# One kernel, one convolution stage: weights loaded first, folding moved back, eight small casts, row statistics interleaved

## The chip, the core and the metric

One Trainium2 chip, one of its cores. The metric is the device time of one execution in microseconds (us). The engines are TensorE (PE: matmuls, and PEld: its weight loads), VectorE (DVE), ScalarE (ACT), GpSimd (POOL) and SyncE (SP), which here only issues DMAs. Engines run on their own and meet at semaphores.

## What is computed

An audio tower layer on x of 32 x 375 x 256: a strided convolution with a layer norm, then attention with a folded key/value projection, then a mixture of 16 experts beside a shared expert. The change is in the first part and in the preparation of weights for the others:

```python
xb = x.reshape(B, L // 2, 2, D)              # B 32, L padded to 376, D 256
h = einsum('btki,oik->bto', xb, conv_w) + conv_b + xb.mean(axis=2)
h = (h - mean) * rsqrt(var + 1e-5) * ln_gamma + ln_beta
h = h + attention(layernorm(h))              # k and v from ((W_k + W_v) @ W_down_kv) @ W_up_{k,v}
h = h + experts(layernorm(h)) + shared_expert(layernorm(h))
```

## The kernel before

Everything that matters to numbers is multiplied as a split of fp32 into two fp16 numbers: a high part (a copy scaled by 64 for weights) and a low part (the difference). A product takes three matmuls: high by high, low by high, high by low. ScalarE makes the high parts, GpSimd the low parts of the inputs, VectorE the low parts of the weights.

The convolution stage works on 32 batches of 188 rows, each in two tiles of 94 rows. Two batches, so four tiles, are a group g; there are 16 groups. Each tile has one of the eight PSUM banks, so even groups (par 0) use banks 0 to 3 and odd ones banks 4 to 7.

For each tile TensorE runs 13 matmuls (L1397, L1403): one for the bias row, twelve for four chunks of the contraction in three products. It waits for the low part of the batch (`xl_ready`) and until VectorE has read the bank two groups before (`gam_done`).

For each group the engines do, in the order of their programs:

- VectorE (`of_conv`, `of_normal`): four `bn_stats` of the PSUM tiles (L991), four `bn_aggr` (L985), then `stats_ready`; four scalar_tensor_tensor that subtract the mean and multiply by gamma (L999); a reciprocal (L1003). Then for the group two before, once GpSimd has added beta: four `bn_stats` of the normalized rows (L1010), four `bn_aggr`, and a copy of the result into `MV` (L1015). Groups 14 and 15 are done behind the loop.
- ScalarE (`conv_group`): the square root (L767), the high parts of two batches that are four ahead (`high_input`, L745), then, when the reciprocal is there, four scalings by it (L774).
- GpSimd: the low parts of the same two batches (`low_input`, L585), then the addition of beta into `H` (`add_beta`, L580).
- SyncE: the load of a batch into one of four input buffers, as soon as the low part of the batch before it there is made (L438).

Before the first group, SyncE issues constants, five weights of the folding, conv_w, bias, gamma and beta, four input batches, and the other weights, in that order. VectorE adds W_k and W_v, TensorE folds in two steps (L1378, L1383) through ScalarE, and only behind both does the first convolution tile start. VectorE adds half the identity to conv_w (L969), which gives the mean of the two rows.

The weights of the later stages are cast in two pieces. Behind its scalings in group 0 ScalarE makes the high part of 2048 columns, in group 1 that of 3104; VectorE makes the low parts behind its reciprocal of the same group (`low_weights`, L972). SyncE waits for both (`lo_done`) and issues, between the loads of inputs, blanks and tables that later stages need: they lie over the place of the uncast weights.

Of the kernel before, what the change touches and what calls it, by code (L numbers as in the profile page):

```python
# [49 lines left out]
HOT = FIRST + ROUNDS + 8  # L50
QE = 4
# [24 lines left out]
W_ALL = W_SD + 4 * D  # L76

# [28 lines left out]
def build(nc, x_t, conv_w, conv_b, gamma, beta, wq, wk_t, wv_t, wo, w_down, w_up_k, w_up_v, gate, s_g, s_u, s_d,  # L106
# [7 lines left out]
    with ctx:  # L114
# [130 lines left out]

        const_in, weights_in, fold_in, conv_w_in, bias_in = (sem(n) for n in ("const_in", "weights_in", "fold_in", "conv_w_in", "bias_in"))
# [61 lines left out]
        def conv_groups(eng, body):  # L308

            body(0, 0, 0)  # L310
            body(1, 1, 1)
            with eng.Fori(1, B // 4 - 1) as i:
                body(2 * i, 0, 2)
                body(2 * i + 1, 1, 2)
            body(B // 2 - 2, 0, 3)
            body(B // 2 - 1, 1, 3)
# [102 lines left out]
        def _(sp):  # L419
            sp.dma_start(C[:, :], const).then_inc(const_in, 16)  # L420
# [4 lines left out]
            sp.dma_start(WS[:, W_CONV:W_Q].rearrange("p (c n) -> p c n", c=4), conv_w.rearrange("(c p) n -> p c n", p=128)).then_inc(conv_w_in, 16)  # L425
            for dst, src in ((BIAS, conv_b), (GAM, gamma), (BET, beta)):
                sp.dma_start(dst, src.rearrange("(a n) -> a n", a=1).broadcast_to((128, D))).then_inc(bias_in, 16)
            for j in range(RING):
                sp.dma_start(XS[j], x_t[j, :, :]).then_inc(x_in[j], 16)
# [12 lines left out]
            sp.wait_ge(lo_done, 4)  # L442
            sp.wait_ge(fold_copied, 2)
            sp.dma_start(SEL, select).then_inc(blanks_in, 16)
            for par in range(2):
                sp.dma_start(MT[par], blank[:, 0:S]).then_inc(blanks_in, 16)
            for i in range(4, B // RING):
# [124 lines left out]
        def _(pool):  # L572
# [14 lines left out]
            def conv_group(g, par, age):  # L587
                if age < 3:
# [154 lines left out]
        def _(act):  # L743
# [3 lines left out]
            act.wait_ge(m1_done, 1)  # L747
            copy(M1[0:DL, :], bank[0][0:DL, 0:256]).then_inc(m1_copied, 1)
            for i in range(2):
                act.wait_ge(fold_done, i + 1)  # L750
                copy(WS[:, W_K + 512 * i:W_K + 512 * (i + 1)], bank[2 + i][:, :]).then_inc(fold_copied, 1)
            act.wait_ge(half_added, 4)
            copy(WH[:, W_CONV:W_Q], WS[:, W_CONV:W_Q], WSCALE).then_inc(hi_done, 1)
            act.wait_ge(bias_in, 16 * 3)
            act.wait_ge(rows_set, 2)
            copy(BROW[0:1, :], BIAS[0:1, :], WSCALE)
            copy(BHI[32:33, :], BIAS[32:33, :], WSCALE).then_inc(hi_done, 1)
# [7 lines left out]
            def conv_group(g, par, age):  # L765
                act.wait_ge(stats_ready, g + 1)
                nc.scalar.activation(SDB[par][0:HT, :], MVB[par][0:HT, :, 1], ACT.Sqrt, bias=C[0:HT, C_EPS64:C_EPS64 + 1]).then_inc(sd_done, 1)  # L767
                if age < 3:
# [12 lines left out]
            for j in range(RING):  # L781
                high_input(j, j)
            act.wait_ge(fold_copied, 2)
# [175 lines left out]
        def _(dve):  # L959
# [3 lines left out]
            dve.wait_ge(fold_in, 16 * 5)  # L963
            nc.vector.tensor_tensor(WKT, WKT, WVT, ALU.add).then_inc(summed, 1)
            dve.wait_ge(conv_w_in, 16)
            dve.wait_ge(const_in, 16)
# [3 lines left out]
            def low_weights(c0, c1, count):  # L970
                dve.wait_ge(hi_done, count)
                nc.vector.scalar_tensor_tensor(WL[:, c0:c1], WS[:, c0:c1], WSCALE, WH[:, c0:c1], ALU.mult, ALU.subtract).then_inc(lo_done, 1)  # L972

            low_weights(W_CONV, W_Q, 1)
            dve.wait_ge(hi_done, 2)
            nc.vector.scalar_tensor_tensor(BROW[32:33, :], BIAS[32:33, :], WSCALE, BHI[32:33, :], ALU.mult, ALU.subtract).then_inc(lo_done, 1)

# [9 lines left out]
            def of_conv(g, par, age):  # L987
# [7 lines left out]
                if age >= 2:  # L995
                    dve.wait_ge(bet_done, g - 1)
# [8 lines left out]
            def of_normal(g):  # L1005
# [5 lines left out]
                aggregate(ln_chain, STATN, AGGR)  # L1011
                ln_chain.wait()
                keep = MV[0:HT, bass.ts(g, CG), :] if not isinstance(g, int) else MV[0:HT, CG * g:CG * g + CG, :]
                hold(dve)
                ln_chain.mark(nc.vector.tensor_copy(keep, AGGR[0:HT, :, :]))  # L1015

            def conv_group(g, par, age):
                of_conv(g, par, age)
                if age == 0:
                    low_weights(W_Q, W_GATE, 3)  # L1020
                if age == 1:
                    low_weights(W_GATE, W_ALL, 4)
                if age >= 2:
                    of_normal(g - 2)
# [3 lines left out]
            with dve.Fori(0, B // 4 - 1) as i:  # L1028
# [4 lines left out]
            conv_chain.leave(B // 4 - 1)  # L1033
            ln_chain.leave(B // 4 - 1)
            for g in (B // 2 - 2, B // 2 - 1):
                of_normal(g)
# [337 lines left out]
        def _(pe):  # L1374
            mm = nc.tensor.matmul
            pe.wait_ge(summed, 1)
            for c in range(2):
                last = mm(bank[0][0:DL, 0:256], WDN[:, c * DL:(c + 1) * DL], WKT[:, c * 256:(c + 1) * 256], start=c == 0, stop=c == 1)  # L1378
            last.then_inc(m1_done, 1)
            pe.wait_ge(m1_copied, 1)  # L1380
            for i, w_ in enumerate((WUK, WUV)):
                for c in range(2):
                    last = mm(bank[2 + i][:, c * 256:(c + 1) * 256], M1[0:DL, c * 128:(c + 1) * 128], w_[0:DL, :], start=True, stop=True)  # L1383
                last.then_inc(fold_done, 1)

            pe.wait_ge(fold_copied, 2)
            pe.wait_ge(lo_done, 2)
            with pe.Fori(0, B // 4) as i:
                for par in range(2):
                    for j in range(2):  # L1390
                        pe.wait_ge(xl_ready, 4 * i + 2 * par + j + 1)
                        xh, xl = XH[2 * par + j], XL[2 * par + j]
                        for qt in range(2):
                            t = 2 * j + qt
                            pe.wait_ge(gam_done, 2 * CG * i + CG * par + t + 1)
                            to = bank[CG * par + t][0:HT, 0:D]
                            mm(to, ONE16, BROW, start=True, stop=False)  # L1397
                            n = 0
                            for c in range(4):
                                w = slice(W_CONV + c * D, W_CONV + (c + 1) * D)  # L1400
                                x = slice(c * S + qt * HT, c * S + (qt + 1) * HT)
                                for a, w_ in split3(xh[:, x], xl[:, x], WH[:, w], WL[:, w]):
                                    last = mm(to, a, w_, start=False, stop=n == 11)  # L1403
                                    n += 1
                            last.then_inc(conv_done, 1)
# [381 lines left out]
```

## Time and profile before

| | |
|---|---|
| time, median of 3 runs | 1866.77 us (1864.56 to 1869.98) |
| span of the profiled execution, first to last instruction | 1863.2 us |
| TensorE busy, of the span | 1690.4 us (91%) |
| VectorE, GpSimd, ScalarE busy | 1227.8, 949.9, 903.4 us |
| convolution stage, its last VectorE copy ends | 148.96 us |
| mean granted TensorE clock | 0.961 |

The profiled execution's own time is given only as its span; the three runs were timed without the profiler. An instruction row of a timeline gives the start in us from the span's start, the duration in us, engine, line, operation, what it writes and reads with partitions x elements, how many were merged (xN), and in brackets how long the engine was idle before and what ended that.

### The profile page before, as it was taken

The page shows a single profiled execution, that of the slowest core. Times are in us where ns is not written, and L with a number is a line of the kernel's source. Part 1 is how long each engine was busy: PE and PEld are TensorE (multiplying, and loading weights), DVE is VectorE, ACT ScalarE, POOL GpSimd, SP SyncE. Part 2 cuts the span into 40 slices and gives each one's busy share as a digit, 9 for nine tenths or more (in the row PEclk, how much of TensorE's full clock was granted, in tenths as well). Part 3 has the DMA queues.
Part 4 walks back from the last instruction along what each step waited for, and adds up shares of the span by engine and source line. Part 5 has one row for each costly group of instructions (what it writes and reads, how often), then busy time and mean ns, then how long its engine had stood idle before and what let it go on. Part 6 is the DMA issues. An engine that isn't in the chain of part 4 may idle for free.

```text
span 1863.2 us, 46732 instructions
## 1 busy us (share of the span) xinstructions
PE 1690.4 (91%) x15566; PEld 1233.5 (66%) x15566; DVE 1227.8 (66%) x3755; ACT 903.4 (48%) x1965; POOL 949.9 (51%) x945
## 2 busy tenths in 40 slices
PE   6874899999999998579999679999999999999997
PEld 5873566666666665357777557777777777777775
DVE  3883778888888888475778665555555555555551
ACT  4442556666666665344234454444444444444442
POOL 3771244444444443372224244666666666666675
PEclk9995999999999999889999779999999999999999
DMA  5532555555655565242110152333333333343422
GB/s 183 171 106 46 110 121 118 133 124 131 126 135 121 133 134 123 59 128 48 34 32 28 42 182 84 100 103 102 99 93 93 99 97 100 102 102 99 101 34 28
DMA packets 220233, 186.52 MB, mean 100 GB/s; under 512 B 165624, under 2 KB 200952, under 8 KB 214008
## 3 DMA queue, kind: packets, MB, share of 16 engines
q1 hardware_dynamic: 193272, 141.11, 28.7%
q0 software_dynamic: 26880, 44.36, 11.6%
q8 instruction: 48, 0.79, 0.2%
q14 instruction: 33, 0.27, 0.1%
HBM read 134.49 MB, written 50.44 MB: 99 GB/s over the span
## 4 chain that ended last, share of the span: by engine, by line
PE 66%; DVE 9%; issue 8%; POOL 5%; SPq 4%; DMA 4%; ACT 1%; DVEq 0%; POOLq 0%; ACTq 0%
PE psum L1698 26%; PE psum L1715 14%; PE psum L1563 6%; PE psum L1583 4%; SPq L466 3%; DVE arena L1101 3%; DVE psum L1109 2%; PE psum L1519 2%; PE psum L1462 2%; PE psum L1416 2%; PE psum L1484 2%; DMA arena<-inverse_sums 2%; PE psum L1430 2%; POOL hidden L580 2%; POOL arena L585 1%
## 5 line engine op out<-in xcount | busy, mean ns | idle before, releaser
L644 POOL TENSOR_TENSOR arena<-arena 128x376 f16<-128x376 f32 x320 | 316.8, 992 | 352.9 <-ACT arena L745 351.4
L1698 PE MATMUL psum<-arena,hidden 128*128 128x376 f16 x3072 | 493.8, 323 | 0.9 <-DVE arena L1337 0.9
L1698 PEld LDWEIGHTS psum<-arena,hidden 128*128 128x128 f16 x3072 | 301.2, 98 | 189.4 <-issue 2.3
L745 ACT ACTIVATE arena<-arena 128x376 f16<-128x376 f32 (+5 forms) x610 | 287.2, 474 | 55.7 <-DVE arena L1273 45.7
L1101 DVE CUSTOM_DVE_ANT_0 arena<-psum,constants 128x188 f32<-128x188 f32 x768 | 227.8, 345 | 107.8 <-PE psum L1416 106.5
L941 ACT ACTIVATE arena<-psum 128x376 f32<-128x376 f32 x256 | 123.9, 484 | 342.7 <-PE psum L1698 342.7
L745 ACT ACTIVATE arena<-psum 128x188 f32<-128x188 f32 (+7 forms) x457 | 168.5, 399 | 237.1 <-PE psum L1678 58.0
L1347 DVE SCALAR_TENSOR_TENSOR arena<-psum,arena 128x376 f32<-128x376 f32 x256 | 140.7, 550 | 185.4 <-ACT arena L941 184.0
L1715 PE MATMUL psum<-hidden,arena 128*128 128x256 f16 (+1 forms) x2304 | 256.6, 273 | 0.0
L1715 PEld LDWEIGHTS psum<-hidden,arena 128*128 128x128 f16 (+1 forms) x2304 | 229.9, 103 | 21.7
L1329 DVE SCALAR_TENSOR_TENSOR hidden<-arena,hidden 128x512 f16<-128x512 f32 x192 | 210.1, 1098 | 8.8 <-ACT hidden L745 8.8
L794 ACT ACTIVATE arena<-psum 128x564 f32<-128x564 f32 x256 | 164.1, 641 | 102.9 <-PE psum L1430 101.4
L602 POOL TENSOR_TENSOR arena<-arena 128x376 f16<-128x376 f32 x128 | 115.5, 902 | 170.7 <-ACT arena L745 164.9
L1109 DVE TENSOR_TENSOR psum<-psum,constants 128x564 f32<-128x564 f32 x256 | 191.1, 747 | 7.4 <-PE psum L1441 7.3
L690 POOL DMA_INDIRECT out<-hidden,arena x96 | 149.8, 1561 | 45.2 <-DVE hidden L1357 23.1
L1357 DVE TENSOR_SCALAR hidden<-psum,arena 128x256 f32<-128x256 f32 x96 | 46.3, 482 | 164.8 <-PE psum L1715 164.5
L1563 PE MATMUL psum<-arena,weights_hi 128*128 128x376 f16 x512 | 136.9, 328 | 1.2 <-DVE arena L1140 1.2
L1430 PE MATMUL psum<-arena 128*128 128x188 f16 x768 | 106.1, 247 | 26.6 <-DVE psum L1109 20.6
L1462 PE MATMUL psum<-arena 128*32 128x188 f32 (+1 forms) x2048 | 125.2, 332 | 4.6 <-ACT arena L794 0.8
L1416 PE MATMUL psum<-arena 96*128 96x188 f16 x768 | 108.3, 251 | 23.3 <-DVE arena L1101 14.3
L681 POOL DMA_INDIRECT arena<-token_table,arena x96 | 110.5, 1151 | 26.8 <-POOL arena L674 11.9
L745 ACT ACTIVATE hidden<-arena 128x512 f16<-128x512 f32 x192 | 118.3, 620 | 5.9 <-DMA arena<-e_g 3.6
(156 smaller groups left out, 2651.4 us busy)
## 6 DMA issues: line engine op xcount, KB each, us to landing
arena<-q_halves SPq DMA_DIRECT2D x384, 47.0 KB, 2.5
arena<-k_halves SPq DMA_DIRECT2D x384, 47.0 KB, 2.3
arena<-e_g SPq DMA_DIRECT2D x16, 1024.0 KB
arena<-e_u SPq DMA_DIRECT2D x16, 1024.0 KB, 5.1
arena<-e_d SPq DMA_DIRECT2D x16, 1024.0 KB
arena<-x_t SPq DMA_DIRECT2D x32, 376.0 KB, 3.5
weighed<-arena POOLq DMA_DIRECT2D x32, 376.0 KB, 4.0
q_halves<-arena SPq DMA_DIRECT2D x32, 188.0 KB, 3.3
```

The costliest lines, as they stand in the source:

```text
L644: nc.gpsimd.tensor_tensor(dst, f, hi, ALU.subtract).then_inc(ready, 1)
L690: nc.gpsimd.indirect_dma_start(out[:, :], bass.IndirectOffsetOnAxis(ap=IDXS[par][0:n, m:m + 1], axis=0), EO[par][0:n, m * D:(m + 1) * D], ...
L745: return nc.scalar.activation(dst, src, ACT.Copy, scale=scale)
L794: nc.scalar.activation(PT[i % RING], TB[i % 2], ACT.Exp).then_inc(exp_done, 1)
L1101: last = nc.vector.tensor_tensor_reduce(out=SC[t], in0=SB[t], in1=C[:, C_DECAY + t * S:C_DECAY + (t + 1) * S], scale=1.0, scalar=-3e38, op ...
L1109: nc.vector.tensor_tensor(TB[j % 2], TB[j % 2], C[:, C_DECAY:C_DECAY + 3 * S], ALU.mult).then_inc(multiplied, 1)
L1329: nc.vector.scalar_tensor_tensor(WEL[par][:, c], WST[:, c], WSCALE, WEH[par][:, c], ALU.mult, ALU.subtract).then_inc(wl_ready[i], 1)
L1416: last = mm(SB[t], QD[cpar][0:2 * KR, i * CW + t * 128:i * CW + (t + 1) * 128], KX[cpar][0:2 * KR, i * S:(i + 1) * S], start=True, stop=True)
L1462: last = mm(OB[32 * k:32 * k + 32, :], V[cpar][p0:p0 + rows, v:v + 32], PT[a % RING][p0:p0 + rows, t * S:(t + 1) * S], start=n == 0, stop= ...
L1563: last = mm(bank[2 * (m % 2) + i][:, 0:CHUNK], w_, a, start=n == 0, stop=n == 5)
L1698: last = mm(bank[2 * (s % 2) + i][:, 0:CHUNK], w_, a, start=n == 0, stop=n == 5)
L1715: last = mm(bank[down_bank[m]][0:rows, 0:D], a, w_, start=n == 0, stop=n == 23)
```

## The change

- SyncE issues only the identity columns of the constants first (new semaphore `ident_in`), then batch 0, conv_w, bias, gamma, beta, batches 1 to 3, the rest of the constants, the folding's weights, and the others. value_rows goes with the first blanks; the wait for the casts moves behind the loads of i == 5, ahead of the blanks for QD and KD.
- The folding goes behind the first group's matmuls, in banks 6 and 7, in three pieces between tiles of group 1. ScalarE keeps the results in group 0.
- The 5152 other columns are cast in `CASTS = 8` pieces of 644, one in each of the groups 2 to 9 (age 2).
- VectorE issues the `bn_stats` and `bn_aggr` of the normalized rows right behind those of the convolution, ahead of the gamma pass. The copy into `MV` becomes a maximum of AGGR with itself and stands between the gamma pass and the reciprocal.

```diff
 SyncE
-            sp.dma_start(C[:, :], const).then_inc(const_in, 16)
+            sp.dma_start(C[:, C_ID:C_ONES], const[:, C_ID:C_ONES]).then_inc(ident_in, 16)
+            sp.dma_start(XS[0], x_t[0, :, :]).then_inc(x_in[0], 16)
+            sp.dma_start(WS[:, W_CONV:W_Q].rearrange("p (c n) -> p c n", c=4), conv_w.rearrange("(c p) n -> p c n", p=128)).then_inc(conv_w_in, 16)
...
             for i in range(4, B // RING):
                 load_x(i)
-                for par in range(2):
-                    v = (*QD, *KD, *V)[2 * (i - 4) + par] if i < 7 else None
-                    if v is not None:
-                        sp.dma_start(v, value_rows if i == 6 else blank).then_inc(blanks_in, 16)
+                if i == 5:
+                    sp.wait_ge(lo_done, 2 + CASTS)
+                if i in (5, 6):
+                    for v in (QD, KD)[i - 5]:
+                        sp.dma_start(v, blank).then_inc(blanks_in, 16)
 ScalarE, conv_group
+                if age == 0:
+                    keep_fold(0)
                 act.wait_ge(inv_ready, g + 1)
                 for t in range(CG):
                     v = LN[par][0:HT, t * D:(t + 1) * D]
                     nc.scalar.activation(v, v, ACT.Copy, scale=RSB[par][0:HT, t:t + 1]).then_inc(scale_done, 1)
-                if age == 0:
-                    act.wait_ge(weights_in, 16 * 6)
-                    copy(WH[:, W_Q:W_GATE], WS[:, W_Q:W_GATE], WSCALE).then_inc(hi_done, 1)
-                if age == 1:
-                    copy(WH[:, W_GATE:], WS[:, W_GATE:], WSCALE).then_inc(hi_done, 1)
+                if age == 0:
+                    keep_fold(1)
+                if age == 1:
+                    act.wait_ge(weights_in, 16 * 6)
+                    act.wait_ge(fold_copied, 2)
+                if age == 2:
+                    copy(WH[:, cast_columns(g)], WS[:, cast_columns(g)], WSCALE).then_inc(hi_done, 1)
 VectorE
+            def normal_stats(g):
+
+                dve.wait_ge(bet_done, g + 1)
+                hold(dve)
+                for t in range(CG):
+                    ln_chain.mark(nc.vector.bn_stats(STATN[t][0:HT, :], H[0:HT, CG * g + t, :]))
+
+            def keep_normal(g):
+
+                keep = MV[0:HT, bass.ts(g, CG), :] if not isinstance(g, int) else MV[0:HT, CG * g:CG * g + CG, :]
+                ln_chain.wait()
+                hold(dve)
+                ln_chain.mark(nc.vector.tensor_tensor(keep, AGGR[0:HT, :, :], AGGR[0:HT, :, :], ALU.max))
+
+            def conv_group(g, par, age):
                 for t in range(CG):
                     dve.wait_ge(conv_done, CG * g + t + 1)
                     hold(dve)
                     conv_chain.mark(nc.vector.bn_stats(STAT[t][0:HT, :], bank[CG * par + t][0:HT, 0:D]))
+                if age >= 2:
+                    normal_stats(g - 2)
                 aggregate(conv_chain, STAT, MVB[par])
+                if age >= 2:
+                    aggregate(ln_chain, STATN, AGGR)
                 conv_chain.wait()
                 dve.sem_inc(stats_ready, 1)
...
                                                    GAM[0:HT, :], ALU.subtract, ALU.mult).then_inc(gam_done, 1)
+                if age >= 2:
+                    keep_normal(g - 2)
                 dve.wait_ge(sd_done, g + 1)
                 hold(dve)
                 nc.vector.reciprocal(RSB[par][0:HT, :], SDB[par][0:HT, :]).then_inc(inv_ready, 1)
...
+                if age == 2:
+                    low_weights(cast_columns(g), g + 1)
 TensorE
+            pe.wait_ge(lo_done, 2)
+            for t in range(CG):
+                conv_tile(0, 0, t)
+            fold_first()
+            for t in range(CG):
+                if t >= 2:
+                    pe.wait_ge(fold_copied, t - 1)
+                conv_tile(0, 1, t)
+                if t < 2:
+                    fold_second(t)
+            with pe.Fori(1, B // 4) as i:
                 for par in range(2):
+                    for t in range(CG):
+                        conv_tile(i, par, t)
```

## Rows read from the trace of the kernel before

**Rows 1.** Timeline of VectorE at the stage's end (columns as above).
```profile
134.46 2.12 DVE L1015 COPY mean_var<-arena 94x8 f32 x1 [0.24 <-DVE arena L985]
...
138.05 0.38 DVE L985 BATCH_NORM_AGGREGATE arena<-arena 94x2 f32<-94x6 f32 x4
...
148.79 0.17 DVE L1015 COPY mean_var<-arena 94x8 f32<-94x8 f32 x1
```

**Rows 2.** Timeline of GpSimd in a steady group.
```profile
95.90 2.34 POOL L580 TENSOR_TENSOR hidden<-arena 94x1024 f32 x1
99.06 3.18 POOL L585 TENSOR_TENSOR arena<-arena 128x752 f16<-128x752 f32 x2 [0.82 <-ACT arena L745]
```

**Rows 3.** Timeline of VectorE in the same group.
```profile
95.93 1.42 DVE L991 BATCH_NORM_STATS2 arena<-psum 94x6 f32<-94x256 f32 x4
...
98.13 1.66 DVE L999 SCALAR_TENSOR_TENSOR arena<-psum,arena 94x256 f32<-94x256 f32 x4 [0.26 <-DVE arena L985]
...
99.79 1.37 DVE L1010 BATCH_NORM_STATS2 arena<-hidden 94x6 f32 x4
...
101.93 0.34 DVE L1015 COPY mean_var<-arena 94x8 f32 x1 [0.24 <-DVE arena L985]
```

**Rows 4.** Timeline of GpSimd at the stage's end.
```profile
134.22 2.34 POOL L580 TENSOR_TENSOR hidden<-arena 94x1024 f32<-94x1024 f32 x1 [3.82 <-ACT arena L774]
```

**Rows 5.** Chain that ended last, one tile of group 15 (start, us, what).
```profile
126.95 1.32 PE psum L1403 x12
```

**Rows 6.** Timeline of VectorE: aggregates of groups 0 to 2 and the weight casts.
```profile
28.55 0.38 DVE L985 BATCH_NORM_AGGREGATE arena<-arena 94x2 f32<-94x6 f32 x4
...
35.52 3.57 DVE L972 SCALAR_TENSOR_TENSOR weights_lo<-arena,weights_hi 128x2048 f16<-128x2048 f32 x1 [4.55 <-ACT weights_hi L745]
...
40.58 0.38 DVE L985 BATCH_NORM_AGGREGATE arena<-arena 94x2 f32<-94x6 f32 x4
...
47.38 3.50 DVE L972 SCALAR_TENSOR_TENSOR weights_lo<-arena,weights_hi 128x3104 f16<-128x3104 f32 x1 [4.45 <-ACT weights_hi L745]
...
52.36 0.38 DVE L985 BATCH_NORM_AGGREGATE arena<-arena 94x2 f32<-94x6 f32 x4
```

**Rows 7.** Timeline of GpSimd beside those casts.
```profile
34.59 2.35 POOL L580 TENSOR_TENSOR hidden<-arena 94x1024 f32<-94x1024 f32 x1
...
45.28 2.36 POOL L580 TENSOR_TENSOR hidden<-arena 94x1024 f32<-94x1024 f32 x1
```

**Rows 8.** Timeline of all engines, from the start to the first convolution matmul.
```profile
3.95 0.58 SPq L425 DMA_DIRECT2D arena<-conv_w  x1
...
7.83 1.97 PE L1378 MATMUL psum<-arena 128*64 128x256 f32 x4 [7.83 <-DVE arena L964]
...
8.77 0.90 DVE L969 SCALAR_TENSOR_TENSOR arena<-constants,arena 128x128 f32<-128x128 f32 x4 [0.99 <-DMA arena<-conv_w]
...
10.27 3.77 PE L1383 MATMUL psum<-arena 64*128 64x256 f32 x8 [0.47 <-ACT arena L745]
...
15.65 1.23 DVE L972 SCALAR_TENSOR_TENSOR weights_lo<-arena,weights_hi 128x1024 f16<-128x1024 f32 x1 [5.99 <-ACT weights_hi L745]
...
19.02 0.44 PE L1397 MATMUL psum<-arena 128*94 128x256 f16 x1 [4.98 <-POOL arena L585]
```

**Rows 9.** Timeline of ScalarE: high parts of weights.
```profile
14.57 1.05 ACT L745 ACTIVATE weights_hi<-arena 128x1024 f16<-128x1024 f32 x1
...
33.59 1.90 ACT L745 ACTIVATE weights_hi<-arena 128x2048 f16<-128x2048 f32 x1
```

**Rows 10.** Timeline of ScalarE in the steady group of rows 2 and 3.
```profile
97.97 0.30 ACT L767 ACTIVATE arena<-arena,constants 94x4 f32<-94x4 f32 x1 [2.58 <-DVEq L994]
98.17 1.53 ACT L745 ACTIVATE arena<-arena 128x752 f16<-128x752 f32 x2
99.90 1.70 ACT L774 ACTIVATE arena<-arena 94x256 f32<-94x256 f32 x4 [0.20 <-DVE arena L1003]
```

**Rows 11.** DMA issues of the first 150 us (KB each, median us to landing).
```profile
arena<-blank SPq DMA_DIRECT2D x4, 768.0 KB, 5.8
```

More of the change, by code:

```diff
@@ L50 @@
 HOT = FIRST + ROUNDS + 8
+CASTS = 8
 QE = 4
@@ L76 @@
 W_ALL = W_SD + 4 * D
+CAST = (W_ALL - W_Q) // CASTS
+assert CAST * CASTS == W_ALL - W_Q
 class Chain:
@@ L243, in meet @@
             eng.wait_ge(engines_met, met[id(eng)])
+        ident_in = sem("ident_in")
         const_in, weights_in, fold_in, conv_w_in, bias_in = (sem(n) for n in ("const_in", "weights_in", "fold_in", "conv_w_in", "bias_in"))
@@ L311, in conv_groups, with cast_columns @@
             body(1, 1, 1)
-            with eng.Fori(1, B // 4 - 1) as i:
+            with eng.Fori(1, 1 + CASTS // 2) as i:
                 body(2 * i, 0, 2)
                 body(2 * i + 1, 1, 2)
-            body(B // 2 - 2, 0, 3)
-            body(B // 2 - 1, 1, 3)
+            with eng.Fori(1 + CASTS // 2, B // 4 - 1) as i:
+                body(2 * i, 0, 3)
+                body(2 * i + 1, 1, 3)
+            body(B // 2 - 2, 0, 4)
+            body(B // 2 - 1, 1, 4)
+        def cast_columns(g):
+            return bass.ds(W_Q + CAST * (g - 2), CAST)
         def hsplit(ap):
@@ L419, in _ @@
         def _(sp):
-            sp.dma_start(C[:, :], const).then_inc(const_in, 16)
+            sp.dma_start(C[:, C_ID:C_ONES], const[:, C_ID:C_ONES]).then_inc(ident_in, 16)
+            sp.dma_start(XS[0], x_t[0, :, :]).then_inc(x_in[0], 16)
+            sp.dma_start(WS[:, W_CONV:W_Q].rearrange("p (c n) -> p c n", c=4), conv_w.rearrange("(c p) n -> p c n", p=128)).then_inc(conv_w_in, 16)
+            for dst, src in ((BIAS, conv_b), (GAM, gamma), (BET, beta)):
+                sp.dma_start(dst, src.rearrange("(a n) -> a n", a=1).broadcast_to((128, D))).then_inc(bias_in, 16)
+            for j in range(1, RING):
+                sp.dma_start(XS[j], x_t[j, :, :]).then_inc(x_in[j], 16)
+            sp.dma_start(C[:, C_ONES:C_ALL], const[:, C_ONES:C_ALL]).then_inc(const_in, 16)
             for dst, src in ((WKT, wk_t), (WVT, wv_t), (WDN, w_down)):
@@ L424, in _ @@
             sp.dma_start(WUV[0:DL, :], w_up_v).then_inc(fold_in, 16)
[L425 to L429, printed above, removed]
             for o, src, c in ((W_Q, wq, 2), (W_O, wo, 2)):
@@ L441, in _ @@
                 load_x(i)
-            sp.wait_ge(lo_done, 4)
             sp.wait_ge(fold_copied, 2)
@@ L587, in conv_group @@
             def conv_group(g, par, age):
-                if age < 3:
+                if age < 4:
                     for j in range(2):
@@ L745, in copy, with keep_fold @@
                 return nc.scalar.activation(dst, src, ACT.Copy, scale=scale)
-            act.wait_ge(m1_done, 1)
-            copy(M1[0:DL, :], bank[0][0:DL, 0:256]).then_inc(m1_copied, 1)
-            for i in range(2):
+            def keep_fold(i):
                 act.wait_ge(fold_done, i + 1)
[L751 to L757, printed above, removed]
+                copy(WS[:, W_K + 512 * i:W_K + 512 * (i + 1)], bank[6 + i][:, :]).then_inc(fold_copied, 1)
             def high_input(b, j):
@@ L775, in conv_group @@
                 if age == 0:
+                    keep_fold(1)
+                if age == 1:
                     act.wait_ge(weights_in, 16 * 6)
-                    copy(WH[:, W_Q:W_GATE], WS[:, W_Q:W_GATE], WSCALE).then_inc(hi_done, 1)
-                if age == 1:
-                    copy(WH[:, W_GATE:], WS[:, W_GATE:], WSCALE).then_inc(hi_done, 1)
-            for j in range(RING):
+                    act.wait_ge(fold_copied, 2)
+                if age == 2:
+                    copy(WH[:, cast_columns(g)], WS[:, cast_columns(g)], WSCALE).then_inc(hi_done, 1)
+            high_input(0, 0)
+            act.wait_ge(half_added, 4)
+            copy(WH[:, W_CONV:W_Q], WS[:, W_CONV:W_Q], WSCALE).then_inc(hi_done, 1)
+            act.wait_ge(bias_in, 16 * 3)
+            act.wait_ge(rows_set, 2)
+            copy(BROW[0:1, :], BIAS[0:1, :], WSCALE)
+            copy(BHI[32:33, :], BIAS[32:33, :], WSCALE).then_inc(hi_done, 1)
+            for j in range(1, RING):
                 high_input(j, j)
-            act.wait_ge(fold_copied, 2)
+            act.wait_ge(m1_done, 1)
+            copy(M1[0:DL, :], bank[7][0:DL, 0:256]).then_inc(m1_copied, 1)
             conv_groups(act, conv_group)
@@ L961, in _ @@
                 dve.sem_inc(s_, v_)
-            dve.wait_ge(fold_in, 16 * 5)
-            nc.vector.tensor_tensor(WKT, WKT, WVT, ALU.add).then_inc(summed, 1)
             dve.wait_ge(conv_w_in, 16)
-            dve.wait_ge(const_in, 16)
+            dve.wait_ge(ident_in, 16)
             for c in range(4):
@@ L1003, in of_conv @@
                 nc.vector.reciprocal(RSB[par][0:HT, :], SDB[par][0:HT, :]).then_inc(inv_ready, 1)
-            def of_normal(g):
-                dve.wait_ge(bet_done, g + 1)
-                hold(dve)
-                for t in range(CG):
-                    ln_chain.mark(nc.vector.bn_stats(STATN[t][0:HT, :], H[0:HT, CG * g + t, :]))
[L1011 to L1018, printed above, removed]
-                if age == 0:
[L1020 to L1024, printed above, removed]
+                if age == 2:
+                    low_weights(cast_columns(g), g + 1)
             conv_group(0, 0, 0)
             conv_group(1, 1, 1)
-            with dve.Fori(0, B // 4 - 1) as i:
+            with dve.Fori(0, CASTS // 2) as i:
                 conv_chain.enter(i, 4 * CG)
@@ L1032, in _ @@
                 conv_group(2 * i + 3, 1, 2)
-            conv_chain.leave(B // 4 - 1)
-            ln_chain.leave(B // 4 - 1)
-            for g in (B // 2 - 2, B // 2 - 1):
-                of_normal(g)
+            conv_chain.leave(CASTS // 2)
+            ln_chain.leave(CASTS // 2)
+            with dve.Fori(0, B // 4 - 2 - CASTS // 2) as i:
+                conv_chain.enter(i, 4 * CG)
+                ln_chain.enter(i, 4 * CG + 2)
+                conv_group(2 * i + 2 + CASTS, 0, 3)
+                conv_group(2 * i + 3 + CASTS, 1, 3)
+            conv_chain.leave(B // 4 - 2 - CASTS // 2)
+            ln_chain.leave(B // 4 - 2 - CASTS // 2)
+            for g in (B // 2 - 2, B // 2 - 1):
+                conv_group(g, g % 2, 4)
+            for g in (B // 2 - 2, B // 2 - 1):
+                normal_stats(g)
+                aggregate(ln_chain, STATN, AGGR)
+                keep_normal(g)
             ln_chain.wait()
@@ L1375, in _ @@
             mm = nc.tensor.matmul
[L1376 to L1381, printed above, removed]
-                for c in range(2):
-                    last = mm(bank[2 + i][:, c * 256:(c + 1) * 256], M1[0:DL, c * 128:(c + 1) * 128], w_[0:DL, :], start=True, stop=True)
-                last.then_inc(fold_done, 1)
@@ L1386, in _, with fold_first @@
-            pe.wait_ge(fold_copied, 2)
-            pe.wait_ge(lo_done, 2)
-            with pe.Fori(0, B // 4) as i:
-                for par in range(2):
[L1390 to L1405, printed above, removed]
+            def fold_first():
+                pe.wait_ge(summed, 1)
+                for c in range(2):
+                    last = mm(bank[7][0:DL, 0:256], WDN[:, c * DL:(c + 1) * DL], WKT[:, c * 256:(c + 1) * 256], start=c == 0, stop=c == 1)
+                last.then_inc(m1_done, 1)
@@ new lines, in fold_second, with conv_tile @@
+            def fold_second(i):
+                pe.wait_ge(m1_copied, 1)
+                for c in range(2):
+                    last = mm(bank[6 + i][:, c * 256:(c + 1) * 256], M1[0:DL, c * 128:(c + 1) * 128], (WUK, WUV)[i][0:DL, :], start=True, stop=True)
+                last.then_inc(fold_done, 1)
+            def conv_tile(i, par, t):
+                j, qt = divmod(t, 2)
+                if qt == 0:
+                    pe.wait_ge(xl_ready, 4 * i + 2 * par + j + 1)
+                xh, xl = XH[2 * par + j], XL[2 * par + j]
+                pe.wait_ge(gam_done, 2 * CG * i + CG * par + t + 1)
+                to = bank[CG * par + t][0:HT, 0:D]
+                mm(to, ONE16, BROW, start=True, stop=False)
+                n = 0
+                for c in range(4):
+                    w = slice(W_CONV + c * D, W_CONV + (c + 1) * D)
+                    x = slice(c * S + qt * HT, c * S + (qt + 1) * HT)
+                    for a, w_ in split3(xh[:, x], xl[:, x], WH[:, w], WL[:, w]):
+                        last = mm(to, a, w_, start=False, stop=n == 11)
+                        n += 1
+                last.then_inc(conv_done, 1)
```

15 lines of the change are left out of this document (8 added, 7 removed).

## The prediction

> **What bounds the kernel now.** The change touches only the convolution stage, which ends at 148.96 us of the 1863.2 us span (the last copy of [rows 1]); what follows stays as it is, so the sum is made over these 149 us. I read three things: the stage's start, the two groups with a large weight cast, and a steady group, each as an engine's timeline.
>
> A steady group takes 6.3 us here: GpSimd adds beta from 95.90 and has the next group's low inputs done, and is free for the next addition, at 99.06 + 3.18 = 102.24 [rows 2]. In [rows 3] VectorE is nearly always at work: statistics of the convolution, gamma pass, statistics of the normalized rows. The last row shows what closes the cycle: a copy of 94x8 values takes 0.34 us and ends at 102.27, just when those low inputs have ended [rows 2]. In [rows 1] the same copy takes 2.12 us and ends at 136.58; GpSimd's operation of [rows 4] ends at 136.56. It waits for GpSimd to be done. TensorE is nearly as full: a tile is 1.32 us of twelve matmuls and 0.11 of the bias one, so 5.7 us a group [rows 5].
>
> The same hold is seen on the weight casts [rows 6, 7]. The 2048-column low part starts at 35.52 and ends at 39.09; GpSimd's addition ends at 36.94, and 2.15 us remain, 1.05 ns a column. The 3104-column one ends at 50.88, 3.24 us after GpSimd's 47.64, again 1.04 ns. With GpSimd idle, 1024 columns took 1.23 us [rows 8]. So a VectorE operation with two inputs in SBUF stands still while GpSimd's runs. Before it VectorE had waited 4.55 and 4.45 us for ScalarE: ScalarE casts only after scaling its four tiles. From aggregate to aggregate these groups took 12.03 and 11.78 us (28.93, 40.96, 52.74, [rows 6]).
>
> I write M(g) for the end of the convolution's aggregates in group g. Before: M(0) = 28.93, M(2) = 52.74, M(15) = 138.43, stage end 10.53 later.
>
> **Start: earlier weights.** conv_w was issued at 3.95, and its first use was at 8.77 [rows 8], 4.8 us later. Now it is third in SyncE's queue, issued near 1.8; between 4.0 and 4.8 us to landing I take 4.3: 6.1. Then as before: identity added 0.90, high part 1.05 [rows 9], low part 1.23 [rows 8], about 0.4 for the bias row and 0.2 of hand-overs: TensorE starts at 9.9 instead of 19.02. Cold start and first group took 28.93 - 19.02 = 9.9, so M(0) = 19.8.
>
> **Folding moved.** It comes behind the first group. Its twelve fp32 matmuls took 1.97 + 3.77 us at the 1.2 GHz level [rows 8]; now TensorE is at its 2.4 GHz level and I take half, 2.9. Group 1 then ends on TensorE at 18.7 + 2.9 + 5.7 = 27.3, and its aggregates 1.1 later. ScalarE, which first keeps M1 and then both folds between its own steps, is ready for the last tile at about the same time. I take M(1) = 28.6. Group 2 adds 5.7 of TensorE, the last statistic and 1.37 of row statistics, and the aggregates: M(2) = 35.8. Bounds 33 to 39. So at M(2) the new kernel is 16.9 us ahead: 9.1 from the start, the rest because groups 0 and 1 no longer cast.
>
> **The eight small casts.** Groups 2 to 9 each cast 644 columns. Their order is that of before: in one group ScalarE scales four tiles, casts, and only then VectorE forms the low part; the next group's statistics are queued behind it on VectorE, and TensorE's banks and ScalarE's square root behind those. Step by step from M:
> - gamma pass to 1.6 (1.66 with its overlap, no pause before it now) [rows 3];
> - ScalarE: square root at -0.1, high inputs to 1.6, which lets GpSimd's two low inputs run from 1.0 to 2.6 and on to 4.2, as [rows 2, 10] lie now;
> - the operation that replaces the copy, a maximum of two SBUF inputs, arrives at 1.65. Held by the first low input it ends at 2.7. Bounds: 0.1 unheld, and both low inputs, 2.6. I take 1.0, since the copy, too, got in between two GpSimd operations that stood back to back. Unheld, beta would start at 4.2, when the low inputs end, instead of 4.7 as below: 0.5 less in eight groups and 0.6 in the four late ones, 6 in all, 1881;
> - reciprocal 2.8, ScalarE's scaling to 4.6 (1.70, [rows 10]), cast 0.73 (1.05 - 380 x 0.83 ns, the slope of [rows 9]) to 5.3;
> - GpSimd adds beta from 4.7 to 7.0 (2.35, [rows 2]). The cast's low part arrives at 5.3, is held to 7.0, and takes 0.67 more: 7.7. Unheld it would end at 6.15;
> - convolution statistics, row statistics, two sets of aggregates: 1.35 + 1.37 + 0.75, now without pauses: M(g+1) = M(g) + 11.2.
>
> That is the pattern of the two old casts (12.03 and 11.78), now eight times, and the narrow width saves little since the order and the hold cost most. M(10) = 35.8 + 8 x 11.2 = 125.4. TensorE idles half of each such group. If it falls to 1.2 GHz for a whole group, that is twice 5.7 = 11.4 us, and it runs a group ahead: hidden, except in the rival below.
>
> **Groups from 10 on.** SyncE now waits for the eighth cast before it issues two 768 KB blanks and, behind them, the inputs of group 10. The cast ends at M(9) + 7.7, 3.5 us before M(10). A blank lands in 5.8 us [rows 11], and the input follows: ScalarE gets it some 3.3 us late. GpSimd, TensorE and VectorE follow, and TensorE restarts after a pause. Over two groups I take 17.2 instead of 12.6 us, 4.6 lost (bounds 0 and 8). Groups 12 and 13: the hold remains, pauses go: 2.8 + 1.35 + 1.37 + 0.75 = 6.3 each. Group 14 loads no input, so the maximum goes unheld: 5.4. M(15) = 125.4 + 17.2 + 12.6 + 5.4 = 160.6.
>
> **Tail.** Both last row statistics still wait for GpSimd's beta, and one maximum is held by it: 8.4 instead of 10.5 us ([rows 1]: 138.43 to 148.96). Stage end 169.0.
>
> **Sum.** Three pieces: -16.9 us at M(2); from M(2) to M(15) 160.6 - 35.8 = 124.8 against 138.43 - 52.74 = 85.7, so +39.1; tail -2.1. Together +20.1 us, and the stage ends at 169.0. The span becomes 1883; the median of the runs shown lies 3.6 us above the profiled span, so 1866.8 + 20 = 1887 us.
>
> **Rivals.**
> - *Held nowhere, and the blanks hidden (faster).* If two-input operations run beside GpSimd, the maximum costs 0.1, and a cast group is 1.85 + 1.7 + 0.73 + 0.85 + 3.5 = 8.6. Eight of them give back 20.8 us, the late groups 2.4: 1864, or 1859 if the blanks hide as well. The place is the cast groups; below 8.7 us each the change breaks even, below 8.0 it is measurably faster. Against it: both ends in [rows 6] fit GpSimd's end within 0.02 us.
> - *Starved.* If the maximum waits for both low inputs, 1.6 us more in twelve groups: +19, 1906 us. For it: GpSimd's two stand back to back. Against: the copy got in.
> - *Blanks hidden, holds as forecast.* 4.6 less: 1882.
> - *TensorE slow.* It falls to 1.2 GHz between cast groups and then sets the end of some: 3 to 6 us more, 1890 to 1893.
> - That the change moves nothing would need the cast groups to come at 8.7 us, 2.1 over the mean of before (85.7 / 13 = 6.6); the fixed order alone (scaling, cast, low part) puts VectorE 3.3 us behind its reciprocal.
>
> **How the numbers follow.** Forecast 0.60; held nowhere 0.11 (0.04 faster, 0.07 within the bound); starved 0.09; blanks hidden 0.12; TensorE slow 0.08. About 0.3% (5.6 us) is what a measurement here can tell from no change. To allow for an unseen mistake in the cast groups I move 0.03 from slower to faster and 0.01 to same. Range 1872 to 1899: the forecast with the start's bounds of 3, half a microsecond on each cast group and the blanks' bounds, the hidden blanks and the slow TensorE, 0.60 + 0.12 + 0.08 = 0.8 in all; left out are the held-nowhere case below and the starved one above.
>
> **What would show it.** TensorE's first convolution matmul near 10 us; low parts of 644 columns that last about 2.4 us and end 0.67 after GpSimd's addition; aggregates 11 us apart in groups 2 to 9; maxima of about 1 us; after the eighth cast two blanks and a late input; the stage's end near 169. The prediction is wrong if the low parts last 0.8 us, if ScalarE's cast precedes its scaling, or if the cast groups come at 8 us.

## The result and the profile after

The changed kernel takes 1884.11 us (median of 4 runs, 1880.26 to 1888.71), the kernel before on the same chip 1866.93: ratio 1.0099, 95% interval 1.0082 to 1.0115. It is slower, as forecast: +20 us was forecast, the medians lie 17.2 us apart, and by the ratio it is 18.5. The profiled span is 1886.7 us. The stage ends at 168.49 us, forecast 169.0, before 148.96 [rows 1]; the 19.5 us between the two are, within some 2 us, the whole loss.

First VectorE's timeline in groups 2 and 3, which answers to [rows 6] (start, us, then as before; M(g) is, as in the prediction, the end of the convolution's aggregates in group g):

```profile
37.14 0.62 DVE L1005 BATCH_NORM_AGGREGATE arena<-arena 94x2 f32<-94x6 f32 x8
...
39.34 1.00 DVE L1019 TENSOR_TENSOR mean_var<-arena 94x8 f32 x1
...
43.09 2.30 DVE L988 SCALAR_TENSOR_TENSOR weights_lo<-arena,weights_hi  x1 [2.66 <-ACT weights_hi L759]
...
47.95 0.61 DVE L1005 BATCH_NORM_AGGREGATE arena<-arena 94x2 f32<-94x6 f32 x8
```

M(2) is 37.76, M(3) 48.56: 10.8 us. VectorE stands idle 2.66 us for ScalarE's cast, and the low part then lasts 2.30 us. The timelines of ScalarE and of GpSimd say why:

```profile
37.81 1.53 ACT L759 ACTIVATE arena<-arena 128x752 f16<-128x752 f32 x2
40.46 1.71 ACT L782 ACTIVATE arena<-arena 94x256 f32<-94x256 f32 x4 [1.11 <-DVE arena L1041]
42.07 0.73 ACT L759 ACTIVATE weights_hi<-arena  x1
```

```profile
38.71 3.18 POOL L599 TENSOR_TENSOR arena<-arena 128x752 f16<-128x752 f32 x2 [1.27 <-ACT arena L759]
42.35 2.35 POOL L594 TENSOR_TENSOR hidden<-arena 94x1024 f32 x1 [0.47 <-ACT arena L782]
```

ScalarE's cast waits behind its scalings. VectorE's low part then arrives at 43.09, inside GpSimd's addition; the addition ends at 44.70, and the low part 0.69 us later. The maximum starts 0.63 us into GpSimd's first low input and ends at 40.34, when that one is done. The eight groups 2 to 9 are alike. The list of waits from 40 to 120 us (waiting line, releaser: us in total, times, longest) has the wait for the cast, but not the hold, which is inside the low part's duration:

```profile
DVE weights_lo L988 <- ACT weights_hi L759: 21.1, 8, 2.7
```

TensorE works 62 of these 87 us, at a mean granted clock of 0.82, and runs ahead: VectorE is not once seen waiting for it between 40 and 120 us. The row gives the stretch, its length, then busy us and count of PE, PEld, DVE, ACT and POOL, the clock, the DMA share and GB/s:

```profile
37.80:124.40 86.60, 62.44 (x445) 59.44 (x444) 65.26 (x184) 32.45 (x65) 44.14 (x24) 0.82 0.27 83
```

Where the eighth cast ends (120.92), SyncE issues the blanks and, behind them, the inputs of group 10; ScalarE then gets the input late. TensorE stands idle for 6.75 us, and from 131 to 135 us its granted clock is 0.50, the 1.2 GHz level: the first two tiles behind the pause take 2.80 and 2.04 us, the next ones 1.42. VectorE waits for these tiles, so 2.0 us of the 17.4 from M(10) to M(12) are the lower clock's; this is read from the trace, no run isolates it. Two maxima show both ends of the hold: at 126.08 GpSimd is idle and the maximum takes 0.15 us, and in group 13 it takes 2.71 us. Timelines of SyncE, ScalarE, GpSimd and VectorE, one fence each:

```profile
120.95 0.80 SPq L466 DMA_DIRECT2D arena<-blank  x2
121.79 2.09 SPq L451 DMA_DIRECT2D arena<-x_t  x4
```

```profile
128.84 1.75 ACT L759 ACTIVATE arena<-arena 128x752 f16<-128x752 f32 x2 [4.18 <-DMA arena<-x_t]
```

```profile
148.78 3.19 POOL L599 TENSOR_TENSOR arena<-arena 128x752 f16<-128x752 f32 x2
```

```profile
126.08 0.15 DVE L1019 TENSOR_TENSOR mean_var<-arena 94x8 f32 x1
...
149.27 2.71 DVE L1019 TENSOR_TENSOR mean_var<-arena 94x8 f32 x1
...
168.33 0.16 DVE L1019 TENSOR_TENSOR mean_var<-arena 94x8 f32<-94x8 f32 x1
```

At the start, TensorE's first convolution matmul is at 11.18 us (19.02 before, [rows 8]). The four identity additions, which have two inputs in SBUF, now fall beside GpSimd's first low input, which was not so before. Timelines of VectorE and of GpSimd:

```profile
6.20 1.82 DVE L985 SCALAR_TENSOR_TENSOR arena<-constants,arena 128x128 f32<-128x128 f32 x4 [6.20 <-DMA arena<-conv_w]
```

```profile
5.66 1.60 POOL L599 TENSOR_TENSOR arena<-arena 128x752 f16<-128x752 f32 x1 [4.48 <-ACT arena L759]
```

Taken one by one, the first addition lasts 1.21 us, the other three 0.28 each. The low input ends at 7.26, and the additions 0.76 us behind it: they were held too. In the profiles of all eight experiments, which share this start, the distance is 0.75 or 0.76 us again, while the low input itself starts anywhere from 5.19 to 5.88.

### The profile page after: what moved, and what is told of

It is laid out like the page before. It is cut to its first block, busy times and chain, and to the rows that moved or that the text cites. A ratio compares the mean times of both kernels' runs of the same rounds, so it can differ in the third digit from the quotient of the medians.

```text
span 1886.7 us, 46738 instructions
## 1 busy us (share of the span) xinstructions
PE 1700.6 (90%) x15566; PEld 1241.9 (66%) x15566; DVE 1245.2 (66%) x3761; ACT 903.7 (48%) x1971; POOL 948.2 (50%) x945
## 4 chain that ended last, share of the span: by engine, by line
PE 70%; DVE 13%; issue 7%; DMA 3%; SPq 2%; ACT 2%; POOL 2%; DVEq 1%; POOLq 0%; ACTq 0%
PE psum L1744 26%; PE psum L1761 13%; PE psum L1609 6%; PE psum L1629 4%; DVE arena L1131 3%; DVE psum L1139 3%; PE psum L1508 3%; PE psum L1565 2%; PE psum L1434 2%; PE psum L1476 2%; PE psum L1462 2%; PE psum L1530 2%; PE psum L1487 2%; SPq L480 1%; PE psum L1724 1%
## 5 line engine op out<-in xcount | busy, mean ns | idle before, releaser
L759 ACT ACTIVATE arena<-arena 128x376 f16<-128x376 f32 (+4 forms) x610 | 287.8, 474 | 66.2 <-DVE arena L1303 46.5
L1761 PEld LDWEIGHTS psum<-hidden,arena 128*128 128x128 f16 (+1 forms) x2304 | 230.0, 103 | 21.6
L1139 DVE TENSOR_TENSOR psum<-psum,constants 128x564 f32<-128x564 f32 x256 | 191.1, 746 | 10.8 <-PE psum L1487 10.6
```

The source lines that it names most:

```text
L759: return nc.scalar.activation(dst, src, ACT.Copy, scale=scale)
L1139: nc.vector.tensor_tensor(TB[j % 2], TB[j % 2], C[:, C_DECAY:C_DECAY + 3 * S], ALU.mult).then_inc(multiplied, 1)
L1761: last = mm(bank[down_bank[m]][0:rows, 0:D], a, w_, start=n == 0, stop=n == 23)
```

## The experiments

Ratios are to the kernel before on the same chip; two chips were used, and their medians for the kernel before differ by 3.4 us (1864.84 for the first four experiments, 1868.26 for the other four), so times are compared here through the ratios. For each run the stage's end is given too (148.96 before, 168.49 changed).

**The casts undone.** Behind ScalarE's scalings, and the like on VectorE; SyncE's wait ahead of the blanks becomes one for 4, so the blanks no longer come late either:

```diff
                 if age == 0:
                     keep_fold(1)
-                if age == 1:
                     act.wait_ge(weights_in, 16 * 6)
                     act.wait_ge(fold_copied, 2)
-                if age == 2:
-                    copy(WH[:, cast_columns(g)], WS[:, cast_columns(g)], WSCALE).then_inc(hi_done, 1)
+                    copy(WH[:, W_Q:W_GATE], WS[:, W_Q:W_GATE], WSCALE).then_inc(hi_done, 1)
+                if age == 1:
+                    copy(WH[:, W_GATE:], WS[:, W_GATE:], WSCALE).then_inc(hi_done, 1)
```

> The eight small casts are undone: the other weights are cast in two pieces, 2048 columns in group 0 and 3104 in group 1, as in the kernel before; start, folding, row statistics and maximum stay as changed. Theory (each cast puts its group some 4.4 us behind, by the order scaling, cast, low part and by GpSimd's hold): groups 0 and 1 get longer, M(2) near 47 instead of 37.8, but groups 2 to 9 come at about 6.3 us instead of 10.8; stage end 136 to 140 instead of 168.5, time 1852 to 1856, faster than both. Rival (the loss sits in the interleaved statistics and the maximum, not in the casts): the groups stay near 10 us and the time stays over 1875.

Measured: 1864.35 us, 0.9999 (0.9988 to 1.0010), stage end 147.60. The loss of the changed kernel is gone, so it sat in the eight casts and what hangs on them; but the forecast gain did not come. M(2) is 47.38 as expected, and then most groups take 7.5 us, not 6.3 (M(14) is 134.34, so 7.25 in the mean of twelve). VectorE's timeline of groups 3 and 4, and GpSimd's, show it:

```profile
52.57 0.62 DVE L1005 BATCH_NORM_AGGREGATE arena<-arena 94x2 f32<-94x6 f32 x8
...
54.76 2.70 DVE L1019 TENSOR_TENSOR mean_var<-arena 94x8 f32 x1
...
60.21 0.62 DVE L1005 BATCH_NORM_AGGREGATE arena<-arena 94x2 f32<-94x6 f32 x8
```

```profile
51.96 2.35 POOL L594 TENSOR_TENSOR hidden<-arena 94x1024 f32 x1 [0.47 <-ACT arena L782]
54.27 3.17 POOL L599 TENSOR_TENSOR arena<-arena 128x752 f16<-128x752 f32 x2
```

The maximum ends at 57.46, GpSimd's second low input at 57.44: the maximum was held by both, as in my rival "starved". Ten of the twelve maxima in the loops lasted 2.29 to 2.72 us.

**The cast ahead of the scalings.**

```diff
+                if age == 2:
+                    copy(WH[:, cast_columns(g)], WS[:, cast_columns(g)], WSCALE).then_inc(hi_done, 1)
                 act.wait_ge(inv_ready, g + 1)
                 for t in range(CG):
...
-                if age == 2:
-                    copy(WH[:, cast_columns(g)], WS[:, cast_columns(g)], WSCALE).then_inc(hi_done, 1)
```

> One line moved: ScalarE casts its 644 columns behind the two high inputs and ahead of the four scalings, where it idles 1.1 us for the reciprocal. Theory (fixed order costs most): VectorE's low part no longer waits for ScalarE, arrives 2.9 us behind M and is held only by GpSimd's second low input to 4.25, ends at 4.9 instead of 7.6: groups of 8.1 instead of 10.8 us, -21.6 us, 1862. Rival (the hold alone costs it): the low part would still end behind GpSimd's addition of beta, no gain beyond 2 us.

Measured: 1851.66 us, 0.9931 (0.9913 to 0.9948), stage end 135.69. It gains 33 us at the stage's end, more than the 21.6 expected. VectorE's timeline, then GpSimd's:

```profile
37.44 0.62 DVE L1005 BATCH_NORM_AGGREGATE arena<-arena 94x2 f32<-94x6 f32 x8
...
39.64 1.00 DVE L1019 TENSOR_TENSOR mean_var<-arena 94x8 f32 x1
40.65 0.79 DVE L988 SCALAR_TENSOR_TENSOR weights_lo<-arena,weights_hi  x1
...
44.01 0.62 DVE L1005 BATCH_NORM_AGGREGATE arena<-arena 94x2 f32<-94x6 f32 x8
```

```profile
39.01 3.90 POOL L599 TENSOR_TENSOR arena<-arena 128x752 f16<-128x752 f32 x2 [1.28 <-ACT arena L759]
```

The group takes 6.57 us. I had the low part held by the second low input; instead it runs in 0.79 us right behind the maximum and the reciprocal, and the second low input waits for it: GpSimd's two last 3.90 us instead of 3.18. The edit takes away both the wait for the cast and the hold by beta; the next experiment takes away the hold alone. The order is right as a cause; who holds whom I had wrong.

**Beta behind the low part.**

```diff
                 if age < 4:
                     for j in range(2):
                         low_input(2 * g + RING + j, 2 * par + j)
+                if age == 2:
+                    pool.wait_ge(lo_done, g + 1)
                 add_beta(g, par)
```

> In groups 2 to 9 GpSimd waits for VectorE's low part of the weights before it adds beta; nothing else. Theory (a two-input operation of VectorE stands still beside GpSimd): the low part takes 0.85 us instead of 2.31, groups of 9.3 instead of 10.8, -12 us, 1872. Rival (2.3 us is what such a strided operation of 644 columns costs by itself): it stays at 2.3 us, beta comes later, and the time is the same or up to 5 us longer.

Measured: 1871.04 us, 1.0028 (1.0015 to 1.0041), stage end 156.78. As the theory had it: the low part takes 0.83 us beside an idle GpSimd, and M to M is 9.3 us.

```profile
43.02 0.83 DVE L990 SCALAR_TENSOR_TENSOR weights_lo<-arena,weights_hi  x1 [2.66 <-ACT weights_hi L761]
...
46.40 0.62 DVE L1007 BATCH_NORM_AGGREGATE arena<-arena 94x2 f32<-94x6 f32 x8
```

So the hold is 1.5 us a group, some 12 us in all, and the wait for the cast, 2.66 us, is still there. The two together, 4.2 us, are what moving the cast took off a group (10.8 to 6.57).

**One input instead of two.**

```diff
-                ln_chain.mark(nc.vector.tensor_tensor(keep, AGGR[0:HT, :, :], AGGR[0:HT, :, :], ALU.max))
+                ln_chain.mark(nc.vector.tensor_reduce(keep, AGGR[0:HT, :, :].unsqueeze(3), AX.X, ALU.max))
```

> The maximum of AGGR with itself becomes a tensor_reduce over an axis of length one: same result, one input. Theory (two inputs make it wait for GpSimd): 0.1 to 0.2 us instead of 1.0 (2.7 once); in the cast groups beta then starts when the low inputs end, 0.45 earlier, 3.6 us in all; some 2 to 3 us more in groups 12 and 13; 1878. Rival (eight values in a register-addressed tile cost 1 us whatever the form): no change.

Measured: 1877.86 us, 1.0072 (1.0049 to 1.0094), stage end 163.92, 4.6 less than changed. The operation takes 0.15 us in the same place, and the low part, now 2.68 us, waits for the same addition of beta, which starts a little earlier:

```profile
39.23 0.15 DVE L1019 TENSOR_REDUCE mean_var<-arena 94x8 f32 x1
...
42.11 2.68 DVE L988 SCALAR_TENSOR_TENSOR weights_lo<-arena,weights_hi  x1 [2.65 <-ACT weights_hi L759]
```

Groups 12 and 13 now take 5.7 us each. So the eight values wait as a tensor_tensor of two inputs and not as a tensor_reduce of one. One input alone is not the rule: the copy of the kernel before has one input too, and was held for 2.12 us [rows 1, 4].

**The blanks spread.** Each blank is issued once the pieces of weights under it are cast:

```diff
-                if i == 5:
-                    sp.wait_ge(lo_done, 2 + CASTS)
-                if i in (5, 6):
-                    for v in (QD, KD)[i - 5]:
+                if i >= 5:
+                    for v, pieces in (((QD[0], 1), (QD[1], 4)), ((KD[0], 6),), ((KD[1], 8),))[i - 5]:
+                        sp.wait_ge(lo_done, 2 + pieces)
                         sp.dma_start(v, blank).then_inc(blanks_in, 16)
```

> The changed kernel, but the four blanks for QD and KD no longer stand together behind the wait for the eighth cast: each is issued behind the loads of inputs once the pieces that lie under it are cast (1 and 4 pieces at i == 5, 6 at i == 6, 8 at i == 7). Theory (the blanks hold back the inputs of group 10 and TensorE pauses): from M(10) to M(12) some 12 to 13 us instead of 17.4; 4 to 5 us less, 1879 to 1880. Rival (that time is something else, such as the new loop that starts there): no change.

Measured: 1883.52 us, 1.0081 (1.0061 to 1.0100), stage end 164.14. By times alone it can't be told from the changed kernel (the intervals overlap). By the profiles M(10) to M(12) takes 13.5 us (123.93 to 137.40) instead of 17.4 (124.38 to 141.75), and ScalarE no longer waits there. One maximum in these two groups is held for 2.70 us, which takes back part of the gain. The 4 us are shown in the trace only.

**Start and folding alone.** Two casts, row statistics apart and the copy, as in the kernel before, in the new start. Of the edit, the part on the statistics:

```diff
-                if age >= 2:
-                    normal_stats(g - 2)
                 aggregate(conv_chain, STAT, MVB[par])
-                if age >= 2:
-                    aggregate(ln_chain, STATN, AGGR)
...
+                if age >= 2:
+                    of_normal(g - 2)
```

> The kernel before with only the new start, the folding behind the first group and its tables' DMAs: casts in two pieces, row statistics apart and the copy, all as before. Theory: TensorE starts near 11 us instead of 19, M(2) near 47.5 instead of 52.7, and steady groups of 6.46 us as before: 1860 to 1862, 5 us faster than before. If the interleaved statistics with a maximum held 2.7 us every other group are a loss, it is 2 to 4 us faster than e1_two_casts (1864). Rival (the interleaving helps by its fewer pauses): slower than e1_two_casts.

Measured: 1859.55 us, 0.9948 (0.9928 to 0.9968), stage end 141.55. M(2) is 45.38 instead of 52.74, and that 7.4 us is kept to the stage's end. The gain by time, 9 us, is more than the 5 expected; M(2) had come 2 us earlier than expected. Against the two-cast version above the stage ends 6 us earlier: interleaved statistics with a held maximum are a loss.

**The three mended together.** Cast ahead of the scalings, tensor_reduce, blanks spread; of the three diffs above, the lines that carry them:

```diff
+                if age == 2:
+                    copy(WH[:, cast_columns(g)], WS[:, cast_columns(g)], WSCALE).then_inc(hi_done, 1)
                 act.wait_ge(inv_ready, g + 1)
...
+                ln_chain.mark(nc.vector.tensor_reduce(keep, AGGR[0:HT, :, :].unsqueeze(3), AX.X, ALU.max))
...
+                    for v, pieces in (((QD[0], 1), (QD[1], 4)), ((KD[0], 6),), ((KD[1], 8),))[i - 5]:
```

> The changed kernel with three edits: cast ahead of the scalings, tensor_reduce instead of the maximum, blanks spread. Theory, added up from the parts: e2_cast_before_scaling at 1851.7; cast groups 6.3 instead of 6.57 us, -2; blanks -6; groups 12 and 13 at TensorE's 5.7, -2: 1842, 22 us faster than before. Rival (the gains overlap, since TensorE's 5.7 us is the floor): 1846.

Measured: 1844.68 us (1837.66 to 1846.98), 0.9860 (0.9833 to 0.9887), stage end 126.08. It beats both kernels. Its median lies between the theory's 1842 and the rival's 1846, but these were reckoned from times on the other chip. Against the kernel before on its own chip it is 23.6 us faster by the medians; the theory had 22, the rival some 19, which is a ratio of 0.990 and just outside the interval. So the theory is favoured, by a narrow margin. VectorE's timeline:

```profile
36.76 0.62 DVE L1004 BATCH_NORM_AGGREGATE arena<-arena 94x2 f32<-94x6 f32 x8
...
38.95 0.15 DVE L1018 TENSOR_REDUCE mean_var<-arena 94x8 f32 x1
...
39.89 0.83 DVE L987 SCALAR_TENSOR_TENSOR weights_lo<-arena,weights_hi  x1 [0.70 <-ACT weights_hi L758]
...
43.27 0.62 DVE L1004 BATCH_NORM_AGGREGATE arena<-arena 94x2 f32<-94x6 f32 x8
...
125.92 0.16 DVE L1018 TENSOR_REDUCE mean_var<-arena 94x8 f32<-94x8 f32 x1
```

Cast groups come at 6.5 us, not 6.3: the low part now waits 0.7 us for the cast.

**Two casts and one input.** The two-cast version, and

```diff
-                ln_chain.mark(nc.vector.tensor_tensor(keep, AGGR[0:HT, :, :], AGGR[0:HT, :, :], ALU.max))
+                ln_chain.mark(nc.vector.tensor_reduce(keep, AGGR[0:HT, :, :].unsqueeze(3), AX.X, ALU.max))
```

> e1_two_casts with the tensor_reduce instead of the maximum. Theory (e1 lost its gain to the maximum, held for 1.0 to 2.7 us in twelve groups; unheld, VectorE needs some 5.3 us a group and TensorE's 5.7 sets the pace): groups 2 to 13 of 5.7 instead of 7.25 us, -18 us, 1846. Rival (the groups of e1 are slow for another cause, such as the order of statistics and gamma pass): no change beyond 3 us.

Measured: 1847.52 us, 0.9889 (0.9871 to 0.9907), stage end 130.79. Most groups come at 5.68 us, TensorE's pace (VectorE's timeline):

```profile
59.42 0.62 DVE L1005 BATCH_NORM_AGGREGATE arena<-arena 94x2 f32<-94x6 f32 x8
...
65.10 0.62 DVE L1005 BATCH_NORM_AGGREGATE arena<-arena 94x2 f32<-94x6 f32 x8
```

VectorE now waits for TensorE's last tile, ten times up to 0.6 us between 60 and 120 us. The maximum alone was worth 16.8 us of stage there (147.60 to 130.79), where groups are tight, and 4.6 in the changed kernel, where the casts cover it. Against start and folding alone (141.55) the stage ends 10.8 us earlier, so interleaved statistics pay once the keeping operation is not held; how much of this the order gives and how much the tensor_reduce in place of the copy, no run parts. Eight well placed casts end the stage 4.7 us earlier than these two (126.08), but by time the intervals of the two runs overlap.

## Why the prediction was right, and where it was not

- **Start.** First convolution matmul forecast at 9.9, measured 11.18. The term that failed is the identity additions at 0.90 "as before": the new order puts batch 0 first, GpSimd's low input falls beside them, and they took 1.82. This is the very hold that I used elsewhere and left out here. ScalarE's bias row waited 0.73 us for beta, of which 0.35 reached VectorE. M(0) was 20.54 against 19.8.
- **M(2).** 37.76 against 35.8, 2.0 late: 0.7 from the start; folding 0.4, since it took 1.08 and twice 1.13 us, 3.3 against 2.9; and 0.8 in which TensorE waited, 0.32 and 0.45 us, for the kept folds, behind 1.18 us in which ScalarE waited for the next inputs to land. The lead at M(2) was 15.0 us, not 16.9. The granted clock reads 1.00 over both foldings, so the 1.2 GHz level that I gave the old one rests on its pace alone.
- **Eight casts.** The step that decides, and it held: 10.8 us a group against 11.2, the stations within 0.3 us of where they were put: cast at M + 4.3, beta until M + 6.9, low part until M + 7.6. Undoing the casts takes the loss away; delaying beta takes the hold away (1.5 us a group), moving the cast takes the 2.66 us wait and the hold away. Most of the four tenths is the shorter way from low part to aggregates (3.2 us, where I had 3.5).
- **Blanks.** M(10) to M(12) took 17.37 us, forecast 17.2; the late input is seen (4.18 us of wait), and spreading the blanks gave 3.9 us back. I had no price for the restart; here two tiles at the 1.2 GHz level made up 2.0 us of it, so that the figure came out within 0.2 is partly luck.
- **Groups 12 and 13.** Forecast 6.3 each; 5.95 and 7.53. The term that failed is the maximum's 1.0 us in groups that follow closely: it was held 2.71 us in group 13. In the changed kernel this happened once, so it cost 1.2 us; in the two-cast version it ate 17 us, and my expectation there was off by 10.
- **Tail.** 8.3 us from M(15) = 160.17, forecast 8.4.
- **The sum.** The stage's end is off by 0.5 us, and part of that is luck: 2.0 us too early at M(2), 3.0 too long over the eight casts, 0.2 too short over the blanks, 0.4 too short over groups 12 to 14, 0.1 too long in the tail.
- **The range.** The bounds that it names add up to 1875 and 1897, not to 1872 and 1899; the result lies inside either.
- **The rivals.** "Held nowhere" fell with the 2.30 us low parts. "Starved" was right for the mechanism where GpSimd works without a gap, and wrong for the eight cast groups, where GpSimd idles before its low inputs. "TensorE slow" was right nowhere but in the 2.0 us behind the blanks; in the cast groups VectorE waited for TensorE not once, though the mean granted clock was 0.82.

The rule of the Trainium skill that the prediction weighed ("SBUF — State Buffer", "Who interferes with whom") held for the eight values too: a maximum of two SBUF inputs took 1.00 us beside GpSimd's low inputs and 0.15 with GpSimd idle. The page gives no size; "whatever its size" was my reading of that.

## What to carry to other kernels

Splitting a large piece of side work into many only helps if each piece fits where its engine waits anyway: here each of eight pieces paid the same ordered chain (scaling, cast, low part) that the large ones had paid twice. Look for the idle time in the engine's own row, put the piece there, and the same eight pieces turn a loss of 18 us into a gain of 13. When a VectorE operation is to run beside GpSimd, look at its form and its SBUF inputs, not at its elements: of eight values the maximum of two inputs was held here, the copy of one input as well, and of these three forms only the tensor_reduce ran free. And when an order of loads is changed, ask which operations now meet: the identity additions doubled their time that way.

## What the runs showed of the hardware

- When a two-input VectorE operation meets GpSimd's operations, who waits does not follow from who came first alone. Where GpSimd had been idle before its first low input, the maximum got in between the two low inputs every time (0.99 to 1.01 us in the cast groups of the changed kernel). Where GpSimd came into them straight from its addition, the maximum waited for both in 15 of 17 cases over these runs, 2.3 to 2.7 us, and in the two others for one (1.02 us). The point of arrival alone does not part them: 0.62 or 0.63 us into the first low input in the cast groups, 0.48 to 0.92 in the second, 0.62 in the two exceptions. What decides stays open; no run was made for it.
- A VectorE operation that follows another closely can keep GpSimd out: with the cast moved, the low part went right behind the maximum and GpSimd's pair took 3.90 us instead of 3.18.
- A held operation shows as a long duration and not as a wait: the low part reads 2.30 us in the trace, with 0.83 us of work, so the list of waits leaves it out.
